# Router logits taken as extra columns of two projections, and an output projection in two interleaved halves

## The reference, cut to what matters

```python
def attn(x):                                  # 4096 tokens x 512, 8 heads of 128, blocks of 128 tokens
    q, k, v = x @ Wq.T, x @ Wkv.T             # q and k l2-normalised per head, scaled
    attn = softmax(mask(q*8 @ k.T))           # own block and the one before
    o = attn @ v * sigmoid(x @ Wg.T + bg)     # a gate per head
    return o @ Wo.T
x = layernorm(x + attn(x))                    # x2, no learned scale
scores = softmax(x2 @ gate_w.T)               # 8 experts
weights, idx = top_k(scores, 2)
y = sum over the 2 experts of w * (silu(x2 @ w1.T) * (x2 @ w3.T)) @ w2.T
z = the same with the shared expert (ws1, ws3, ws2)
x = layernorm(x2 + y + z)
```

## Time and profile before

| | |
|---|---|
| median of 3 runs | 1851.13 us (1848.14 to 1852.72) |
| time of the profiled execution | 1852.04 us |
| its span, first to last instruction | 1850.3 us |
| mean granted TensorE clock | 0.959 of full |
| PE busy | 1673.7 us, 90% of the span |
| PEld busy | 1353.9 us, 73% |
| DVE busy | 845.5 us, 46% |
| ACT busy | 656.9 us, 36% |
| POOL busy | 600.4 us, 32% |

### The profile page before, as it was taken

One profiled execution on the slowest core, in us unless ns is written; L12 is line 12 of the kernel. 1 busy time (PEld: TensorE's weight loads), 2 busy tenths in 40 slices (PEclk: granted clock), 3 DMA queues, 4 the chain that ended last, 5 costly groups with the idle time before them and its releaser, 6 DMA issues.

```text
span 1850.3 us, 29848 instructions
## 1 busy us (share of the span) xinstructions
PE 1673.7 (90%) x8950; PEld 1353.9 (73%) x8951; DVE 845.5 (46%) x1991; ACT 656.9 (36%) x1558; POOL 600.4 (32%) x689
## 2 busy tenths in 40 slices
PE   5999999999999999999999997656699999999860
PEld 4888888888888888888888886434477777777630
DVE  6554554544545545545545543722322222222476
ACT  4343343333433433433433432212233333333332
POOL 4232232232332332332332321266234444444111
PEclk9999999999999999999999998888899999999985
DMA  6000001000000000000000001365733233233796
GB/s 218 7 18 29 23 17 28 23 17 28 23 17 28 23 17 28 23 17 28 23 20 26 23 24 68 121 136 121 207 121 103 102 102 102 98 107 109 245 314 241
DMA packets 81976, 139.92 MB, mean 76 GB/s; under 512 B 10428, under 2 KB 27396, under 8 KB 81940
## 3 DMA queue, kind: packets, MB, share of 16 engines
q1 hardware_dynamic: 66852, 101.54, 17.6%
q0 software_dynamic: 13600, 37.90, 6.2%
q10 hardware_dynamic: 1488, 0.04, 0.0%
HBM read 97.89 MB, written 41.56 MB: 75 GB/s over the span
## 4 chain that ended last, share of the span: by engine, by line
PE 60%; issue 20%; DMA 7%; DVE 7%; POOL 3%; ACT 2%; SPq 1%; DVEq 0%; POOLq 0%; ACTq 0%
PE bank L1003 20%; PE bank L935 12%; PE bank L964 7%; PE bank L1070 6%; PE bank L1086 5%; DMA z_d<-eo 5%; PE bank L1059 2%; PE bank L910 2%; POOL rnorm L610 2%; PE bank L1046 2%; DVE pp L1256 1%; PE bank L945 1%; PE bank L1031 1%; PE bank L1015 1%; PE bank L1093 1%
## 5 line engine op out<-in xcount | busy, mean ns | idle before, releaser
L1003 PE MATMUL bank<-wh,xh 128*128 128x512 f32 (+2 forms) x896 | 338.2, 377 | 18.7 <-DVE wl L1185 11.9
L1003 PE MATMUL bank<-wl,xh 128*128 128x512 f32 (+2 forms) x896 | 327.1, 365 | 0.0
L1003 PE MATMUL bank<-wh,xl 128*128 128x512 f32 (+2 forms) x896 | 327.0, 365 | 0.0
L610 POOL TENSOR_TENSOR rnorm<-ssmax,nhalf 128x4 f32<-128x4 f32 x128 | 133.1, 1040 | 526.7 <-DVE ssmax L1220 523.5
L1003 PEld LDWEIGHTS bank<-wh,xh 128*128 128x128 f32 x896 | 169.8, 190 | 51.4 <-DVE qkn L1227 15.6
L1003 PEld LDWEIGHTS bank<-wh,xl 128*128 128x128 f32 x896 | 169.6, 189 | 28.5
L1003 PEld LDWEIGHTS bank<-wl,xh 128*128 128x128 f32 x896 | 170.1, 190 | 23.9
L1206 DVE TENSOR_TENSOR bl<-bank,bh 128x512 fp32r<-128x512 f32 x104 | 71.8, 691 | 180.4 <-ACT bh L749 180.2
L1227 DVE TENSOR_TENSOR qkn<-bank,rnorm 128x512 f32<-128x512 f32 x128 | 88.5, 692 | 130.3 <-POOL rnorm L610 130.3
L772 ACT ACTIVATE pp<-pp,nmx 128x256 f32<-128x256 f32 x256 | 127.1, 498 | 35.9 <-DVE nmx L1261 35.8
L910 PEld LDWEIGHTS bank<-ident,bx 128*128 128x128 f32 x416 | 52.5, 146 | 117.6 <-DMA bx<-x_d 74.2
(11 more groups left out here) (187 smaller groups left out, 3587.0 us busy)
## 6 DMA issues: line engine op xcount, KB each, us to landing
fs<-in_w13T SPq DMA_DIRECT2D x18, 512.0 KB, 6.2
xt<-in_xT SPq DMA_DIRECT2D x33, 256.0 KB, 3.2
xr<-in_x SPq DMA_DIRECT2D x32, 256.0 KB, 2.6
x_d<-xr SPq DMA_DIRECT2D x32, 256.0 KB, 2.0
bx<-x_d SPq DMA_DIRECT2D x32, 256.0 KB, 5.1
ga<-eo_d SPq DMA_DIRECT2D x16, 512.0 KB, 5.4
gb<-eo_d SPq DMA_DIRECT2D x16, 512.0 KB, 6.3
out<-oo SPq DMA_DIRECT2D x32, 256.0 KB, 2.3
```

Of the source, the lines that this page charges most:

```text
L610: pool.tensor_tensor(rnorm[:, :], ssmax[:, :], nhalf[:, :], ALU.pow).then_inc(rn_s, 1)
L1003: mm = pe.matmul(b[:, 0:n], a[:, par, c, :], wt[:, c, cols], start=(c == 0 and k == 0), stop=(c == DC - 1 and k == 2))
```

## The change

The logits are linear in x2 before the layernorm, which is x + o @ Wo.T. So gate_w becomes 8 more columns of the projection weights (v2 is now 272 columns wide) and its product with Wo becomes 8 more columns of `woh` and `wol`. The residual tile `xr` gets 8 more columns that hold x's part of the logits, the residual add adds the other part, and the layernorm's normalisation is applied to all 520 columns. gate_w is first centred (its mean over the 512 inputs taken off, by `sum_gate` on TensorE and one DVE instruction), so that the mean of x2 drops out. The product of gate_w and Wo is made once, on TensorE in step 1 (`gate_of_wo`, 32 matmuls of 8 columns in plain float32, before `turn_p` 0), from an untransposed copy of Wo of 2 MB that SP loads in step 0.

The output is now 520 columns wide and is held in two PSUM banks: `project_out` makes for each of the 24 stationary blocks two matmuls, 264 columns into psA[1] and then 256 into psY. DVE adds the halves in two instructions with a semaphore count each. `router`, `turn_x2`, x2h, x2l and their waits are gone, and so is step 34. DVE has two new small copies a step (x's part of the logits from psY into `xr` at the end of the step; the finished logits out of `xr` behind the normalisation). `k0` now waits for the first half's add, since both use psA[1]. The routing chain is one instruction shorter.

```diff
-NCOL = 3 * H * P + H
-NCOL_ROW = NCOL + 8
+NCOL = 3 * H * P + H + E
+DG = D + E
...
-        woh = sbuf(sa, "woh", [P, H, D], F32R)
-        wol = sbuf(sa, "wol", [P, H, D], F32R)
+        woh = sbuf(sa, "woh", [P, H, DG], F32R)
+        wol = sbuf(sa, "wol", [P, H, DG], F32R)
...
+        wo_n = sbuf(sn, "wo_n", [P, DC, H * P])
...
-        QKV_WIDTH = {"v1": GRP // 2, "v2": GRP // 2 + H}
+        QKV_WIDTH = {"v1": GRP // 2, "v2": GRP // 2 + H + E}
...
-        M_STEP = 19
+        M_STEP = 18
...
-                        sp.wait_ge(x2t_s, s - 1)
-                        settled(sp)
-                    sp.dma_start(xr[:, par, :], x[bass.ds(s * P, P), :]).then_inc(xr_in[par], 16)
+                    sp.dma_start(xr[:, par, 0:D], x[bass.ds(s * P, P), :]).then_inc(xr_in[par], 16)
+                if not middle and s == 0:
+                    sp.dma_start(wo_n[:, :, :], wo.rearrange("(c p) k -> p c k", p=P)).then_inc(wo_n_in, 16)
...
-            act.activation(wh[:, :, 3 * H * P:NCOL], wgs[:, 0, :, :], ACT.Copy)
-            act.activation(wgp[:, :, 0, :], wgs[:, 1, :, :], ACT.Copy).then_inc(wg_split, 1)
+            act.activation(wh[:, :, 3 * H * P:3 * H * P + H], wgs[:, 0, :, :], ACT.Copy)
+            act.wait_ge(gate_centred, 1)
+            act.activation(wh[:, :, 3 * H * P + H:NCOL], wgs[:, 1, :, :], ACT.Copy).then_inc(wg_split, 1)
...
-                    act.wait_ge(wo_s, u)
+                    act.wait_ge(wo_s, 2 * u)
...
+                    act.wait_ge(wog_s, 1)
+                    act.activation(woh[:, :, D:DG], psO[:, 0:H * E].rearrange("p (h e) -> p h e", e=E), ACT.Copy)\
+                       .then_inc(wog_hi, 1)
...
-                    act.wait_ge(x2t_s, w + 1)
-                    if middle or w >= 1:
-                        act.wait_ge(lg_s, w)
-                    act.activation(x2h[:, :, :], psT[0][:, :], ACT.Copy).then_inc(x2_hi, 1)
...
-                    if route_on:
-                        pe.wait_ge(lg_read, s - 2)
+                    if s_out:
+                        pe.wait_ge(res_s, 2 * s - 3)
...
-            def router(v, wait_read):
-
-                pe.wait_ge(x2_lo, v + 1)
-                if wait_read:
-                    pe.wait_ge(v_s, 2 * NT)
-                    pe.wait_ge(lg_read, v)
+            def sum_gate():
+
+                pe.wait_ge(ident0, 1)
+                pe.wait_ge(wg_in, 32)
                 for c in range(DC):
-                    for k, a in enumerate((x2h, x2l)):
-                        mm = pe.matmul(psA[1][:, 2 * E:4 * E], a[:, c, :],
-                                       wgp[:, c, :, :].rearrange("p a e -> p (a e)"),
-                                       start=(c == 0 and k == 0), stop=(c == DC - 1 and k == 1))
-                mm.then_inc(lg_s, 1)
+                    mm = pe.matmul(psO[:, 0:E], all_ones[:, :], wgs[:, 1, c, :], start=(c == 0), stop=(c == DC - 1))
+                mm.then_inc(gate_sum, 1)
+
+            def gate_of_wo():
+
+                pe.wait_ge(wo_n_in, 16)
+                pe.wait_ge(gate_centred, 1)
+                for h in range(H):
+                    for c in range(DC):
+                        mm = pe.matmul(psO[:, h * E:(h + 1) * E], wo_n[:, c, h * P:(h + 1) * P], wgs[:, 1, c, :],
+                                       start=(c == 0), stop=(c == DC - 1))
+                mm.then_inc(wog_s, 1)
...
-                    elif b == 0 and first is None:
-                        pe.wait_ge(x2_lo, u - 1)
-                        pe.wait_ge(ptev, 4 * u)
...
-                    pe.wait_ge(res_s, w)
+                    pe.wait_ge(res_s, 2 * w)
                 else:
                     pe.wait_ge(w_lo, NW)
 
                 if gated:
                     pe.wait_ge(z_read, w + 2)
                     pe.wait_ge(v_s, 2 * w + 4)
+                halves = ((psA[1][:, 0:DG - D // 2], slice(D // 2, DG)), (psY[:, 0:D // 2], slice(0, D // 2)))
                 for h in range(H):
                     for k, (a, b) in enumerate(((oh, woh), (oh, wol), (ol, woh))):
-                        mm = pe.matmul(psY[:, :], a[:, h, :], b[:, h, :], start=(h == 0 and k == 0),
-                                       stop=(h == H - 1 and k == 2))
-                mm.then_inc(wo_s, 1)
-
-            def turn_x2(w, par):
-                pe.wait_ge(x2_s, w + 1)
-                for c in range(DC):
-                    mm = pe.transpose(psT[0][:, c * P:(c + 1) * P], xr[:, par, c * P:(c + 1) * P], ident[:, :])
-                mm.then_inc(x2t_s, 1)
+                        for out, cols in halves:
+                            mm = pe.matmul(out, a[:, h, :], b[:, h, cols], start=(h == 0 and k == 0),
+                                           stop=(h == H - 1 and k == 2))
+                            if h == H - 1 and k == 2:
+                                mm.then_inc(wo_s, 1)
...
+                if u_first:
+                    gate_of_wo()
...
+            dve.wait_ge(gate_sum, 1)
+            dve.scalar_tensor_tensor(out=wgs[:, 1, :, :], in0=psO[:, 0:E].unsqueeze(1).to_broadcast([P, DC, E]),
+                                     scalar=-1.0 / D, in1=wgs[:, 1, :, :], op0=ALU.mult, op1=ALU.add)\
+               .then_inc(gate_centred, 1)
             weight_low(0)
...
-                dve.tensor_tensor(zb[:, :], psY[:, GRP // 2:GRP // 2 + H], bgb[:, :], ALU.add).then_inc(z_read, 1)
+                dve.tensor_tensor(zb[:, :], psY[:, GRP // 2:GRP // 2 + H], bgb[:, :], ALU.add)
+                if not early:
+                    dve.wait_ge(lg_read, s - 1)
+                dve.tensor_copy(xr[:, par, D:DG], psY[:, GRP // 2 + H:GRP // 2 + H + E]).then_inc(z_read, 1)
...
-                    dve.wait_ge(wo_s, w + 1)
+                    dve.wait_ge(wo_s, 2 * w + 1)
                     dve.wait_ge(xr_in[par], 8 * (w - par) + 16)
-                    dve.tensor_tensor(xr[:, par, :], psY[:, :], xr[:, par, :], ALU.add).then_inc(res_s, 1)
-                    dve.wait_ge(res_s, w + 1)
-                    layernorm_stats(xr[:, par, :], w, bn_s, mv_s, ve_s, None if w_first else rstd_s)
+                    dve.wait_ge(z_read, w + 1)
+                    dve.tensor_tensor(xr[:, par, D // 2:DG], psA[1][:, 0:DG - D // 2], xr[:, par, D // 2:DG], ALU.add)\
+                       .then_inc(res_s, 1)
+                    dve.wait_ge(wo_s, 2 * w + 2)
+                    dve.tensor_tensor(xr[:, par, 0:D // 2], psY[:, 0:D // 2], xr[:, par, 0:D // 2], ALU.add)\
+                       .then_inc(res_s, 1)
+                    dve.wait_ge(res_s, 2 * w + 2)
+                    layernorm_stats(xr[:, par, 0:D], w, bn_s, mv_s, ve_s, None if w_first else rstd_s)
...
+                    dve.wait_ge(x2_s, w + 1)
+                    dve.tensor_copy(logits[:, bass.ds(w, 1), :], xr[:, par, D:DG].unsqueeze(1)).then_inc(lg_read, 1)
...
+                    dve.wait_ge(wog_hi, 1)
+                    dve.tensor_tensor(wol[:, :, D:DG], psO[:, 0:H * E].rearrange("p (h e) -> p h e", e=E),
+                                      woh[:, :, D:DG].bitcast(F32), ALU.subtract).then_inc(wog_lo, 1)
...
-                    dve.wait_ge(x2_hi, w + 1)
-                    if not w_first:
-                        dve.wait_ge(lg_s, w)
-                    dve.tensor_tensor(x2l[:, :, :].rearrange("p c n -> p (c n)"), psT[0][:, :],
-                                      x2h[:, :, :].rearrange("p c n -> p (c n)").bitcast(F32), ALU.subtract)\
-                       .then_inc(x2_lo, 1)
...
-            chained(dve.tensor_tensor(shifted, logits[:, :, 0:E], logits[:, :, E:2 * E], ALU.add))
-            chained(dve.tensor_reduce(r_m[:, :], shifted, AX_X, ALU.max))
-            chained(dve.tensor_tensor(shifted, shifted, per_tile(r_m[:, :]), ALU.subtract))
+            chained(dve.tensor_reduce(r_m[:, :], logits[:, :, :], AX_X, ALU.max))
+            chained(dve.tensor_tensor(shifted, logits[:, :, :], per_tile(r_m[:, :]), ALU.subtract))
```

More of the change, by code:

```diff
@@ L132, in block_kernel @@
         ol = sbuf(sa, "ol", [P, H, P], F32R)
-        x2h = sbuf(sa, "x2h", [P, DC, P], F32R)
-        x2l = sbuf(sa, "x2l", [P, DC, P], F32R)
+        sbuf(sa, "to_the_end_of_wo_n", [P, H, P])
         stage = [pp[:, :, :].rearrange("p h (a c) -> p (h a c)", c=GRP // 2).rearrange("p (c n) -> p c n", n=GRP),
@@ L320, in in_steps @@
             step(NT + 1, 1)
-            step(NT + 2, 0)
         def settled(eng):
@@ L1106, in step @@
                     pe.wait_ge(consts, 11)
+                if first:
+                    sum_gate()
                 if proj_on:
@@ L1109, in step @@
                 if attn_on:
-                    turn_qk(u, 0, None if (middle or s >= 3) else u_first)
-                if route_on:
-                    if proj_on:
-                        pe.wait_ge(v_s, 2 * s)
-                    router(s - 3, not proj_on)
+                    turn_qk(u, 0, u_first)
                 if out_on:
@@ L1124, in step @@
                 if proj_on:
-                    project(s, "k0", par, first, route_on)
```

(1 more changed line is left out.)

82 lines of the change are left out of this document (40 added, 42 removed).

## The result

| | before | after |
|---|---|---|
| median | 1851.33 us (4 runs, 1848.14 to 1852.72) | 1821.23 us (4 runs, 1816.28 to 1824.72) |
| ratio | | 0.9838, 95% interval 0.9811 to 0.9865 |
| time of the profiled execution | 1852.04 us | 1820.34 us |
| its span | 1850.3 us | 1818.3 us |
| mean granted clock | 0.959 | 0.955 |

The change makes the kernel 1.6% faster. The forecast was 1819 us.

What follows compares the result with a forecast made beforehand. PE was taken to bound the middle steps, so work removed from it outside two waits shortens the span. The terms summed to -32.9 us from 1852.04, forecast 1819 us, range 1811 to 1832.

Steps and rivals of the forecast that it cites:

- part 8: At the start, DVE's first weight subtraction waits for the sum over gate_w: +0.8 us, between 0 and +2.1.
- part 9: `gate_of_wo` in step 1, between k1 and `turn_p` 0: 64 records at 0.111 us, +7.1 us.
- part 7: Steps 33 and 34: `project_out` starts earlier at full clock, routing -7.8 us; last line, routing chain one instruction shorter, -0.5 us.
- Part 1: `router` removed from steps 3 to 31: 0.90 us each, -26.1 us.
- Part 2: `turn_x2` transposes removed from steps 2 to 31: 0.35 us each, -10.5 us.
- Part 3: `project_out` as 48 matmuls: a pair costs 0.2399 us, 0.15 us a step more, +4.6 us.
- Part 5: Residual add in two: the second ends where the one ended, 0 us; the new small copies are covered.
- rival A: The residual add lengthens the chain to `scores` 1 and v0: 0.3 us a step, +9 us, 1828 us; chance 0.14.
- rival B: `gate_of_wo` runs slow, by its clock or more than two loads a matmul: +7 to +9 us; chance 0.16.
- C (bank): PE pays for changing the output bank at every matmul of `project_out`: 123 us, about 1941 us; chance 0.05.
- D (load): Each block's second weight load in `project_out` is dropped or free: -5 us, 1814 us; chance 0.05.
- E: `project_out`'s wait for the output's low part replaces router and transposes: 1856 us, not faster; chance 0.02.

Runs made afterwards that it cites:

- e4_instr_back: The changed kernel with PE's share of the router and transposes put back, without their ACT and DVE copies: 1865.8 us, ratio 1.0064 against the kernel before.
- e8_add_slow: The changed kernel with one more DVE instruction over 256 columns between the two residual adds, result unused: 1833.6 us, ratio 0.9883 against the kernel before.
- e1_grouped: The changed kernel with the halves of `project_out` one after the other instead of in turn on each block: 1812.3 us, ratio 0.9777 against the kernel before.
- e11_best_stats: The combined kernel (grouped halves, `gate_of_wo` in pieces, earlier first weight subtraction) with layernorm statistics in two halves: 1795.7 us, ratio 0.9686 against the kernel before.
- e3_spread: The changed kernel with `gate_of_wo` in four pieces of 8 matmuls, behind `scores` 0, k0, q1 and k1: 1818.9 us, ratio 0.9821 against the kernel before.
- e7_quarter: The changed kernel with only 8 of the 32 `gate_of_wo` matmuls, logits wrong, for timing alone: 1808.1 us, ratio 0.9756 against the kernel before.
- e5_apart: The changed kernel with the output projection split as 512 and 8 columns instead of 256 and 264: 1901.2 us, ratio 1.0247 against the kernel before.

## Why the prediction was right, and where its terms were not

The time, the sign and the mechanism were right, but two errors of size and one of chance stood against each other. Profile against profile, cut at points that both traces have:

| stretch | predicted | measured |
|---|---|---|
| start to `turn_qk` 0 of step 1 (part 8) | +0.8 | 43.65 - 41.90 = +1.75 |
| from there to `values` 0 of step 1 (part 9) | +7.1 | +12.09 |
| 30 steps, to `values` 0 of step 31 (parts 1 to 5) | -30.7 | 1000.47 - 1033.95 = -33.48 |
| step 32 (part 6) | -1.8 | 26.98 - 28.56 = -1.58 |
| `values` 0 of step 32 to routing (part 7) | -7.8 | 21.21 - 28.94 = -7.73 |
| routing to the end (part 7, last line) | -0.5 | 689.92 - 692.97 = -3.05 |
| span | -32.9 | -32.0 |

- Part 1, the router: 0.90 us a step, and 0.90 when put back (e4_instr_back).
- Part 2, the transposes: mis-sized. 0.35 us was the distance to the next start; taken out they gave 0.43, put back they cost 0.45, since the matmuls on both sides of them also shift. Over 30 steps that is 2.4 us more gain than forecast.
- Part 3, the halves: 0.15 us a step forecast, 0.17 measured. A pair at 0.2396 against the 0.2399 worked out from v1 and v2.
- Part 5, the residual add: the second add ends 0.84 us behind the next matmul's start where the one ended 0.89 behind the earlier trace rows. That is close to the forecast of no gain and no loss; the distance from k0 to `scores` 1 came out 0.05 us a step shorter, another 1.5 us of gain. e8_add_slow shows what the rival A would have cost, 0.33 us a step for one instruction of 0.35; that a shortening pays as well, e1_grouped. The statement that both waits belong to this chain is shown for `scores` 1 alone: the wait at v0 stayed near 8 us in both of these kernels, and fell only in e11_best_stats, where `scores` 1 no longer waited.
- Parts 6 and 7: the end of phase A came out to 0.3 us. The last `project_out` did run at the full clock, which was the open point.
- Part 8: 1.24 us at q0 where I took 0.8, and by the end of the prologue 1.75 and 1.18 in two profiles.
- Part 9 failed in size: two records a matmul, as argued (x64), and 0.111 us each until the clock fell, but 0.213 for the last 27, so 9.90 us instead of 7.1, and 2.0 us in the transposes and v0 behind. That is rival B, to which I gave 0.16 and +7 to +9 us; it came at +5.0. It happened by its first cause, the clock, and e3_spread and e7_quarter show it. The Trainium skill ("TensorE: Matmul & The Clock Gate", Part 1: The HAM clock gate) says that a monitor of how busy the array has been sets the clock; here PE had no idle time in the rows from 64.12 to 74.02 us and the clock fell all the same, so busy time as the profile counts it does not explain the fall. I had argued from `turn_p` and `values`, which keep the full clock in each middle step; but those are short stretches between wide ones.
- The end of the span: -2.6 us beyond the term, which is scatter: phase B took 694.6 us in the second profile of the same kernel. That was luck. Without it the span would have missed the forecast by 3.5 us, still inside the range.

Rivals C (bank) and D (load) are both refuted by the pair's 0.2396 us and by e1_grouped, not only by the total. E did not come about: in the middle steps no wait at `project_out` is listed, in a profile whose step is 1.16 us shorter.

## What to carry to other kernels

A matmul of 8 or 16 columns cost about 0.11 us here, even on the block in use; the same 8 columns were nearly free, 0.006 us a block, as part of matmuls of 264. So fold a thin product into a wide one and split the sum evenly over the banks, and give each half its own consumer early: grouped halves let DVE take the first under the second. A one-off block of thin matmuls did best here in pieces, in a gap and between wide groups, and worse in one row. A listed wait of the weight load is not yet a price: its worth is the distance between PE's starts with and without it. And compare edits at a marker inside the trace that ends the changed part, since the rest of the span may scatter by more than the edit.

## What the runs showed of the hardware that I had not expected

- A row of 8-column float32 matmuls, back to back, let the granted clock fall from 1.00 to 0.50, at about 68 us both in the changed kernel, where the row began at 64.1, and in the one with a wide matmul behind each eight records, where it began at 63.9. Records start 0.11 us apart at the upper level and 0.21 at the lower.
- 48 matmuls that alternate between two banks and 48 that change once take the same time to 0.01 us.
- Taking four transposes out from between other matmuls gave back 0.43 us where the distance from their first start to the next one was 0.35; put back, they cost 0.45.
- A wide matmul starts 0.025 to 0.028 us behind an 8-column one on the same block, but then takes 0.312 to 0.321 us to the next start instead of 0.2335 (e5_apart).
- Which property of the narrow matmuls lowers the clock (8 columns, or the plain float32 form) was not separated: no run has a long row of wide float32 matmuls or of narrow rounded ones.
